# A macaron block (routed FFN, attention, routed FFN) on one core: the first sequence's score stacks built by TensorE instead of through DRAM

## The reference, cut to what matters

```python
x = x + 0.5 * ffn(layernorm(x))
x = x + attn(layernorm(x))          # RMS norm, q k v, causal softmax, Wo, + its own normalised input
x = x + 0.5 * ffn(layernorm(x))

q = (xn @ Wq.T + bq).reshape(B, T, H, hd).transpose(0, 2, 1, 3)     # B, T, H, hd = 8, 256, 16, 8
k = (xn @ Wk.T + bk).reshape(B, T, H, hd).transpose(0, 2, 1, 3)
scores = jnp.einsum('bhqd,bhkd->bhqk', q, k) * scale                # causal mask, softmax, times v
```

## Time and profile before

| | us |
|---|---|
| median of 3 runs | 338.12 |
| the runs | 335.42 to 338.41 |
| the profiled execution | 338.99 |
| its span in the trace | 337.2 |
| PE busy in the span | 247.0 (73%) |
| DVE busy | 215.7 (64%) |
| POOL busy | 178.7 (53%) |
| ACT busy | 141.9 (42%) |

### The profile page before, as it was taken

One profiled execution on the slowest core, in us unless ns is written; L12 is line 12 of the kernel. 1 busy time (PEld: TensorE's weight loads), 2 busy tenths in 40 slices (PEclk: granted clock), 3 DMA queues, 4 the chain that ended last, 5 costly groups with the idle time before them and its releaser, 6 DMA issues.

```text
span 337.2 us, 7298 instructions
## 1 busy us (share of the span) xinstructions
PE 247.0 (73%) x2098; PEld 193.7 (57%) x2098; DVE 215.7 (64%) x689; ACT 141.9 (42%) x343; POOL 178.7 (53%) x318
## 2 busy tenths in 40 slices
PE   0670079999806667989999999997985207999970
PEld 0560069999705343556666666564654107999960
DVE  4887018887617748976767678766544642888760
ACT  3320024444205824866666666874231102444420
POOL 6847603545533201777778678786157720454551
PEclk9999999999956977999999999998565556999995
DMA  7956371331040631752442412200002266133100
GB/s 209 394 231 219 110 186 40 101 100 47 23 114 10 209 119 39 216 163 85 126 151 84 144 51 80 64 5 2 0 33 93 79 174 188 36 106 101 44 20 0
DMA packets 34752, 35.39 MB, mean 105 GB/s; under 512 B 3964, under 2 KB 28673, under 8 KB 34720
## 3 DMA queue, kind: packets, MB, share of 16 engines
q1 hardware_dynamic: 29984, 27.07, 26.4%
q0 software_dynamic: 3008, 6.34, 5.6%
q10 hardware_dynamic: 1728, 1.59, 1.6%
HBM read 20.05 MB, written 15.65 MB: 106 GB/s over the span
## 4 chain that ended last, share of the span: by engine, by line
PE 53%; POOL 16%; issue 9%; DMA 9%; DVE 6%; ACT 2%; SPq 2%; POOLq 1%; ACTq 0%; DVEq 0%
PE bank L1230 13%; PE bank L1241 12%; POOL disp_d L461 6%; PE bank L1379 4%; PE bank L1351 3%; PE bank L1327 3%; DMA disp_d<-row,slot 3%; POOL pT L538 2%; PE bank L1324 2%; PE bank L1222 2%; PE bank L1409 2%; POOL rs L453 2%; PE bank L1191 2%; PE bank L1357 2%; PE bank L1332 1%
## 5 line engine op out<-in xcount | busy, mean ns | idle before, releaser
L704 ACT ACTIVATE pT<-bank 128x512 f32<-128x512 f32 x96 | 56.2, 599 | 42.8 <-PE bank L1357 28.9
L1230 PE MATMUL bank<-xsT,ew 128*128 128x128 f32 x368 | 52.2, 288 | 0.1
L538 POOL TENSOR_SCALAR_AFFINE_SELECT pT<-pT 128x512 f32<-128x512 f32 x64 | 40.9, 641 | 17.6 <-ACT pT L704 17.4
L1241 PE MATMUL bank<-experts,hT 128*128 x368 | 48.8, 276 | 0.0
L1230 PEld LDWEIGHTS bank<-xsT,ew 128*128 128x128 f32 x368 | 48.0, 204 | 0.5 <-issue 0.2
L1014 DVE TENSOR_REDUCE mh<-bank 128x2 f32<-128x512 f32 x64 | 42.0, 683 | 8.6 <-PE bank L1327 8.6
L904 DVE TENSOR_SCALAR hT<-bank,ew 128x128 f32<-128x128 f32 x92 | 28.0, 345 | 28.2 <-PE bank L1230 27.0
L1241 PEld LDWEIGHTS bank<-experts,hT 128*128 128x128 f32 x368 | 44.9, 192 | 0.3 <-issue 0.3
L620 ACT ACTIVATE hT<-bank,ew 128x128 f32<-128x128 f32 x92 | 28.8, 364 | 33.2 <-PE bank L1230 33.2
L469 POOL DMA_INDIRECT out<-ys_sb,xs_sb x23 | 22.5, 980 | 35.7 <-DVE ys_sb L928 35.1
L469 POOL DMA_INDIRECT x_d<-ys_sb,xs_sb x23 | 22.7, 986 | 31.7 <-DVE ys_sb L928 29.2
(11 more groups left out here) (126 smaller groups left out, 457.0 us busy)
## 6 DMA issues: line engine op xcount, KB each, us to landing
sp_d<-spl SPq DMA_DIRECT2D x32, 192.0 KB, 2.6
xs_sb<-disp_d SPq DMA_DIRECT2D x46, 129.0 KB, 2.2
experts<-in_experts SPq DMA_DIRECT2D x8, 578.0 KB, 8.6
qz<-sp_d SPq DMA_DIRECT2D x32, 96.0 KB
ks<-sp_d SPq DMA_DIRECT2D x32, 96.0 KB
disp_d<-pad ACTq DMA_DIRECT2D x12, 129.0 KB, 3.5
row<-in_x SPq DMA_DIRECT2D x4, 256.0 KB, 4.6
row<-x_d SPq DMA_DIRECT2D x4, 256.0 KB, 3.8
```

The source lines that it names most:

```text
L538: pool.affine_select(out=p_, in_=p_, pattern=[[0, 4], [1, P]], compare_op=ALU.is_ge, fill=0.0, base=0, channel_multiplier=-1).then_inc(a_p ...
L704: act.activation(pT[:, u, :], bank[2 + u % 2][:, :], ACT.Exp, scale=SCALE).then_inc(a_e, 1)
L1230: mm = pe.matmul(bank[2 + 2 * (k % 2) + c // 2][:, (c % 2) * P:(c % 2 + 1) * P], ew[:, k % WRING, c * P:(c + 1) * P], xsT[:, k % 2, :], st ...
L1241: mm = pe.matmul(bank[6 + k % 2][:, 0:D], hT[:, k % 2, c, :], w2.rearrange("p a c -> p (a c)"), start=(c == 0), stop=(c == HC - 1))
```

## The change

Sequence 0 no longer goes through DRAM. Its three parts of q and k are kept in a buffer of their own (`spl0`), and PE multiplies them with constant selection matrices `sel` (bfloat16 ones and zeros, 128 x 1344 words, made on the host and loaded by one DMA of 688 KB behind the last tile load of the first routed layer). Each `build` is six matmuls of 256 columns that sum three parts into the rows of the stack, in PSUM; ACT copies the `ks` rows and the second head's `qz` rows to their buffers (two copies per group), DVE the first head's (one copy). There are eight builds: two (k and q) for each of four pairs of head pairs.

- The second head's rows start at 64 instead of 48 (`JOFF`), so the stacks have 112 rows instead of 96, for all sequences.
- SP loses the four stores and eight loads of sequence 0.
- ACT loses `quad_repeat` of units 0, 1 and 2; unit 0 needs none, POOL makes those of units 1 and 2.
- POOL also makes `quad_split3` of unit 2, which DVE made; DVE's `quad_rest(4)` waits for it.
- The v biases of units 0 and 1 are added in one DVE instruction.
- The lists of PE, DVE and ACT are reordered: the score units of half 0 stand among the transposes and products of units 3 and 4. v of unit 3 moves behind all twelve score units.
- Some semaphores are merged; that moves no instruction.

On PE, the builds and the wait for their copies are new:

```diff
+            def build(half, pp, t):
+
+                rows_h = slice(JOFF * half, JOFF * half + JOFF)
+                o = built_from(half, pp, t)
+                for i in range(2):
+                    for n in range(3):
+                        mm = pe.matmul(o[0:SROWS, i * T:(i + 1) * T], sel[rows_h, t, n, 2 * pp + i, :],
+                                       spl0[rows_h, n, t, :], start=(n == 0), stop=(n == 2), **MM_BANK)
+                mm.then_inc(b_mm, 1)
+
+            def copied(n):
+                pe.wait_ge(b_act, 2 * n)
+                pe.wait_ge(b_dve, n)
```

PE's list, from unit 1's v to the first step:

```diff
+            pe.wait_ge(sel_s, 16)
+            pe.wait_ge(q_s2, 1)
+            pe.wait_ge(q_spl, 1)
+            build(0, 0, 1)
+            build(0, 0, 0)
+            quad_qk(2)
+            build(0, 1, 1)
+            pe.wait_ge(q_vc, 1)
+            build(0, 1, 0)
+            copied(1)
+            scores_q(0, 0, 0, 0, 0)
+            scores_q(0, 0, 0, 0, 1)
+            quad_turn(3)
+            quad_v(2)
+            scores_q(0, 0, 0, 0, 2)
+            quad_qk(3)
+            copied(2)
+            scores_q(0, 0, 0, 0, 3)
+            quad_turn(4)
+            scores_q(0, 0, 0, 0, 4)
+            scores_q(0, 0, 0, 0, 5)
             pe.wait_ge(q_Tc, NU)
...
+            build(1, 0, 1)
+            pe.wait_ge(a_mx, 5)
+            build(1, 0, 0)
+            quad_qk(4)
+            pe.wait_ge(q_vc, 2)
+            turn_max(0, 0)
+            pe.wait_ge(b_act, 5)
+            build(1, 1, 1)
+            pe.wait_ge(a_mx, 6)
+            build(1, 1, 0)
+            copied(3)
             scores_q(0, 0, 0, 1, 0)
-            turn_max(0, 0)
+            copied(4)
             for u in range(1, 6):
                 scores_q(0, 0, 0, 1, u)
             pe.wait_ge(a_mtc, 1)
             pe.wait_ge(q_r, NU)
+            quad_v(3)
```

ACT's list:

```diff
             quad_split1(0)
+            quad_split2(0)
             quad_split1(1)
-            quad_split2(0)
-            quad_repeat(0)
             quad_copy(2)
             quad_split2(1)
-            quad_repeat(1)
+            act.wait_ge(static_s, 6)
+            stack_copy(0, 0)
             ln_apply(1, 3)
+            stack_copy(0, 1)
             quad_copy(3)
             quad_split1(2)
             ln_apply(1, 4)
             quad_split2(2)
-            quad_repeat(2)
             quad_copy(4)
             quad_split1(3)
+            stack_copy(1, 0)
             quad_split1(4)
...
             max_copy(0, 0)
+            stack_copy(1, 1)
```

SP's list, and POOL's:

```diff
             tile_loads(0)
+            sp.dma_start(sel_w[:, :], sel_in).then_inc(sel_s, 16)
             all_scattered(0)
...
-            split_stores(0, 1)
-            stack_load(0, 0, 0)
-            stack_load(0, 0, 1)
+            split_stores(1)
             stack_load(1, 1, 0)
+            stack_load(1, 1, 1)
             max_rows(0, 0, 0)
-            stack_load(1, 1, 1)
             split_stores(2)
```

```diff
-            for q in range(NU):
+            for q in range(NU - 1):
                 ln_scale(1, q)
...
+            quad_repeat(1)
+            ln_scale(1, 4)
...
             max_split(0, 0)
+            quad_split3(2)
+            quad_repeat(2)
```

More of the change, by code:

```diff
@@ L101, in constants, with selectors, build @@
     return c
-def build(nc, x_in, wqkvo, cols_in, rows_in, w_gate, experts_in, const_in, out):
+SPLIT_OF = ((0, 0, 0, 1, 1, 2), (1, 0, 2, 0, 1, 0))
+NPH = NPAIR // 2
+def selectors():
+    s = np.zeros((2, 2, HD, NPH, 2, 3, NPH, SROWS), np.uint16)
+    for t in range(2):
+        for c, n in enumerate(SPLIT_OF[t]):
+            for j in range(2):
+                for h in range(HD):
+                    for i in range(NPH):
+                        s[:, j, h, i, t, n, i, JOFF * j + HD * c + h] = 0x3F80
+    return s.reshape(P, -1).view(np.float32)
+SELW = 2 * 3 * NPH * SROWS // 2
+def build(nc, x_in, wqkvo, cols_in, rows_in, w_gate, experts_in, const_in, sel_in, out):
     ctx = ExitStack()
@@ L375, in split_stores @@
                     q, toks = unit_of(b)
[L376 to L380, removed]
+                    sp.wait_ge(*((q_pool, 1), (q_pool, 3), (q_cp, 1), (q_cp, 2))[q - 1])
+                    sp.wait_ge(*((q_spl, 2), (q_pool, 3), (q_spl, 3), (q_spl, 4))[q - 1])
+                    for t, first, last in ((0, spl[:, (q - 1) % SPL, 0:1, 0, toks].broadcast_to((P, 3, T)),
+                                            spl[:, (q - 1) % SPL, 1:4, 0, toks]),
+                                           (1, spl[:, (q - 1) % SPL, 1:4, 1, toks], spl[:, (q - 1) % SPL, 0:3, 1, toks])):
                         dst = sp_d[(2 * b + t) * t_rows:(2 * b + t + 1) * t_rows, :].rearrange(
@@ L1033, in _ @@
             quad_rest(0)
+            quad_split3(0)
             quad_rest(1)
-            quad_split3(0)
+            quad_vbias(0, 1)
+            quad_split3(1)
+            ln_out(3)
+            dve.wait_ge(static_s, 6)
+            stack_copy(0, 0)
             ln_stats(1, 4)
-            ln_out(3)
-            quad_split3(1)
-            quad_vbias(0)
-            quad_vbias(1)
+            max_unit(0, 0, 0)
+            max_unit(0, 0, 1)
+            stack_copy(0, 1)
             ln_out(4)
+            max_unit(0, 0, 2)
+            max_unit(0, 0, 3)
             quad_rest(2)
-            quad_split3(2)
-            quad_vbias(2)
+            max_unit(0, 0, 4)
+            max_unit(0, 0, 5)
+            quad_vbias(2, 2)
+            stack_copy(1, 0)
+            quad_rest(3)
+            stack_copy(1, 1)
+            quad_rest(4)
             def v_spread(b, k):
@@ L1100, in step @@
                             ln_bias(2, b - 5)
-            dve.wait_ge(static_s, 6)
-            for u in range(6):
-                max_unit(0, 0, u)
-            quad_rest(3)
-            quad_rest(4)
             for u in range(6):
@@ L1514, in _ @@
             expert_tiles(1)
-_INS = ["x", "wqkvo", "cols", "rows", "w_gate", "experts", "const"]
+_INS = ["x", "wqkvo", "cols", "rows", "w_gate", "experts", "const", "sel"]
 def kernel(L0_attn_x, L0_attn_norm_w, L0_attn_Wq, L0_attn_bq, L0_attn_Wk, L0_attn_bk, L0_attn_Wv, L0_attn_bv,
@@ L1540 @@
         "const": constants(),
+        "sel": selectors(),
     }
```

158 lines of the change are left out of this document (98 added, 60 removed).

## The result

The changed kernel takes 342.76 us (median of 4 runs, 341.83 to 346.62) against 337.07 for the kernel before; the ratio is 1.0188 [1.0122, 1.0254]. Timed again later it was 342.85 us, 1.0151 [1.0089, 1.0212]. Ratios here are those of the comparison on the same chip, which leaves disturbed runs out, so that they can differ from the quotient of two medians (most for the kernel with the first gap filled, 1.0045 against 1.011). The forecast was 339.8 and a change "within 1%"; the time lies in the stated range, but the kernel is 1.5 to 1.9% slower.

What follows compares the result with a forecast made beforehand. The opening's chain up to the first second-pass score (the handover) was taken as the bound: -0.1 us without the clock, +1.7 with it, so 338.99 became 340.7 profiled and the median 339.8; range 335.5 to 343.2.

Steps and rivals of the forecast that it cites:

- First score, first maximum: Opening, sequence 0: after the builds and unit 2's q and k, DVE's first maximum starts at 114.05 instead of 121.95.
- Half 0: First six maxima, now among work on units 3 and 4: 9.6 us instead of 5.5, ending at 123.6.
- The waits of 0.8 and 1.4: DVE idle in half 0 ahead of its third maximum (0.8 us) and its fourth (1.4 us), behind PE's products.
- These 7.9 us are not kept: The first maximum's 7.9 us lead shrinks to 0.15 by half 1, as units 3 and 4 stand between score units.
- Between the halves, at full clock: From 123.6: PE's 2.4 us wait for ACT, builds, products and DVE copies; `quad_rest(4)` ends at 130.1.
- Half 1 at full clock: Last six maxima take 3.9 us, to 134.0; v of unit 3 follows the last score, handover at 134.2.
- The sum without the clock: Whole opening: first second-pass score (the handover) at 134.2 against 134.28, a change of -0.1 us.
- The clock: PE at half clock: half of a fall at its 2.4 us wait (0.8), all of one in half 1 (1.0); +1.7 us.
- The third rival: Clock falls at 121, stays down until half 1's builds are done: +5.3 us, median 343.4; chance 0.13.
- The waits that were costed at nothing: `sel` transfer, ACT's copies and POOL's work cost 0; POOL's unit 2 split, 2.88 us, covered by 4.3.
- The change is worth what it moves the handover: Handover is the first second-pass score, at 134.28 before; PE's list is full after it, so shifts count one for one.

Runs made afterwards that it cites:

- the first gap filled: Changed kernel plus seven unread matmuls on PE, only ahead of its wait for ACT's copy of unit 4: 341.85 us, 1.0045.
- PE kept busy: Changed kernel plus 14 unread matmuls: seven ahead of PE's wait for unit 4's copy, seven behind half 1's second score unit: 337.55 us, 1.0000; again 337.04, 0.9966.
- the kernel before with its PE kept busy: Kernel before plus unread matmuls: 22 in its DRAM wait, five ahead of the transposed maxima, five behind half 1's second score unit: 334.79 us, 0.9855; again 336.06, 0.9960.
- the two moved calls: Changed kernel with ACT's copy of unit 4 ahead of its unit 2 split, and v of unit 3 behind half 1's second score unit: 337.12 us, 0.9991; again 336.01, 0.9938.
- unit 4's copy first: Changed kernel with ACT's copy of unit 4's transpose moved ahead of its second split of unit 2: 337.30 us, 0.9979.
- split on DVE: Changed kernel with the third split of unit 2 moved from POOL back to DVE: 341.66 us, 1.0128.
- with the added work: Kernel with the two moved calls plus six empty matmuls in the last sequence, where PE waits for POOL's mask: 336.48 us, 0.9895.
- before, first gap only: Kernel before plus 22 unread matmuls on PE, only in its wait for the stacks from DRAM: 336.34 us, 0.9946.
- experiment 9: The two moved calls timed again, 336.01 us, 0.9938; and with six empty matmuls added in the last sequence, 336.48 us, 0.9895.

## Why the prediction was wrong

The steps, in the prediction's own order. Its times have the reload at 96.41, so its opening without the clock was 134.2 - 96.41 = 37.8 us.

- *First score, first maximum.* Forecast 17.6 us behind the reload, measured 18.3. Right in kind, 0.6 us short. The price of a build was taken from two score matmuls, 0.66 us; two builds, the products of unit 2 and two builds more took 113.91 - 109.13 = 4.78 us at full clock, not 4.36. One such run stands in front of half 0, another between the halves.
- *Half 0.* Forecast 9.55 us, measured 9.53 (114.45 to 123.98). The waits of 0.8 and 1.4 came as 1.17 and 1.41. "These 7.9 us are not kept" was right.
- *Between the halves, at full clock.* Forecast 6.5, measured 6.93 with PE kept busy (124.19 to 131.12).
- *Half 1 at full clock.* Forecast 4.1, measured 4.29.
- *The sum without the clock.* 37.8 forecast, 39.1 measured: 1.3 us too low, mostly the builds and products above.
- *The clock: this is the step that failed most.* "I take half of the first and all of the second", 1.8 us, on the assumption that a stretch at half clock lasts 3.4 us as both did in the profile before. The falls came where they were looked for, behind the gap of 2.26 us and in half 1. But the first fall was there in both profiles of the changed kernel, not in half of them, and in one of the two each stretch lasted 6.8 us: 4.6 us in that profile, 2.6 in the other. Had I taken the whole of both falls at 3.4 us, the term would have been 2.7, and the forecast 340.7, still within 1%. It takes the 1.3 us of the line above as well to come out slower: with both, 342.0. In the second profile those 1.3 us are the larger miss, as the clock was only 0.8 short.
- *The third rival* decided "if the granted clock is 0.5 over most of 123 to 130", and in the first profile it was (0.50 from 123.9 to 130.8). Its +5.3 is near the 5.8 of that opening, but in part by luck: the clock cost less than the 5.3, and the 1.3 us made up for it. In the second profile the condition did not hold (0.50 from 126.2 to 129.7), and the kernel was slower all the same. Its argument against ("both earlier stretches ended after 3.4 us with PE at work") rested on two stretches of one execution.
- *The waits that were costed at nothing* cost nothing: the `sel` transfer was issued at 75.76 and the reload stood at 96.19; POOL's split took 2.12 us in place of 2.88.
- *"The change is worth what it moves the handover"* is not shown one for one. The two openings are 5.8 and 3.9 us longer and the medians 5.7 and 4.9, but the spans of these two profiles are longer by 2.9 and 5.4, because the last part, costed at nothing, took 108.2 and 110.9.

The Trainium skill (TensorE: Matmul & The Clock Gate, the table in "Why this matters for your kernels") warns of long idle gaps only; by that rule the clock would have stayed up, since the longest gap is now half of the old one (2.26 us against 5.01). The trace disagrees: the clock fell behind 2.26 us of idle time, and in half 1 behind pieces of 0.39 and 1.38 us. The Trainium skill (TensorE: Matmul & The Clock Gate, "A second HAM failure mode: psum-queue depth-cycling") tells of another kernel whose clock swings because PE pauses often and briefly between groups of matmuls. Half 1 looks like that in both kernels (falls at 131.0 and 134.2 behind short pauses); that it is the same cause is not shown.

What the prediction did not separate is that the kernel before also paid for its clock. With both held at full speed the openings are 35.5 and 39.1 us:

| at full clock, us | before | changed | difference |
|---|---|---|---|
| reload to first maximum | 25.2 | 18.4 | -6.8 |
| first maximum to the end of half 0's work | 4.3 | 9.5 | +5.2 |
| from there to the first maximum of half 1 | 2.8 | 6.9 | +4.1 |
| from there to the handover | 3.2 | 4.3 | +1.1 |

So 6.8 us are won on the DRAM path and 10.4 given back: by units 3 and 4, which used to be worked on during the wait; by the builds of half 1, in a row with DVE's copies; and by v of unit 3 behind the scores. That makes 3.6 us of the loss; the clock, 4.6 or 2.6 us in place of 2.4, makes the rest, 0.2 to 2.2 us.

The best that was run is the kernel before with its PE kept busy (0.9855 and 0.9960); among the changed ones it is the one with the two moved calls (0.9991 and 0.9938), whose opening is 0.9 us longer. By their medians both are about 2% below the changed kernel, and each is below the kernel before by more than the interval in one of its two comparisons.

Open is the last part of the kernel, from the projection of sequence 5 to the end. The clock falls there too, between 232 and 243 us, and in all fourteen profiles the time goes with the length of that stretch at half clock:

| stretch at half clock, us | last part, us | profiles |
|---|---|---|
| 6.8 | 106.6 to 106.9 | changed kernel kept busy, twice; unit 4's copy first |
| 10.2 | 108.2 to 108.8 | changed; split on DVE; two moved calls, twice, and with the added work; before, kept busy |
| 13.7 | 109.2, 109.4 | before, kept busy again; before, first gap only |
| 17.1 | 110.9, 111.0 | before; changed, again; first gap only |

The same kernel has different lengths in two executions (the changed one 10.2 and 17.1), and across the profiles 4.4 us of a time is decided there and not in the opening. That is how the changed kernel kept busy can be level with the kernel before though its opening is 1.2 us longer. What decides the length was not tried beyond experiment 9.

## What to carry to other kernels

When a long wait is taken away, the work that was done during it has to go somewhere: put it, stage by stage, beside the wait's length before counting on the gain. A gap of PE in front of a chain that is PE's own was paid twice here, once as the gap (2.26 us) and once as half clock behind it (3.4 or 6.8 us of it). In such a place count the fall in full, and allow for longer stretches than the ones seen. A few matmuls that nobody reads, put into such a gap, test that theory in one run; here they were also the cheapest fix. And read more than one profile of a kernel before a difference of a few microseconds is given to a cause.

## What was not expected of the hardware

The length of a stretch at half clock was not fixed: 6.8 us twice in one execution of the changed kernel, 3.4 us twice in another of the same program, with PE at work in both, and 6.8 to 17.1 us near the end of the attention. The clock also fell behind gaps of about 1 us in half 1 in three of the changed kernels (as it is, with the first gap filled, with unit 4's copy first), and did not in the kernel with the split on DVE, which has pieces of 0.53, 1.23 and 0.30 us there.
